# An eight-block transformer on one core: another order for the head loop's opening, a rectification shared by two engines, a top-54 threshold searched on unshifted scores

## The reference

```
# block 3, mLSTM: 16 heads, gates from a cumulated log-sigmoid
log_D = log_fg + ig                      # 256 x 256 per head, lower triangle
D = exp(log_D - max_log_D)
C = (q k^T / sqrt(dh)) * D
Cn = C / (max(|C.sum(-1)|, exp(-max_log_D)) + EPS)
h = Cn v                                 # then normalised per head
...
# block 7, attention over 256 keys, 54 scores kept
scores = coef * Q K^T
scores = scores - max(scores, -1)
thr = top_k(scores, 54)[0][..., -1:]
scores = where(scores < thr, -inf, scores)
out = softmax(scores) V @ W_o^T
...
# block 8, MLP with quantised activations and weights
h = bitlinear(h, w1)                     # 256 -> 1024
h = square(relu(h))
return bitlinear(h, w2)                  # 1024 -> 256
```

## Time and profile before

| | |
|---|---|
| median of 3 runs | 565.84 us (562.04 to 568.44) |
| the profiled execution's own time | 569.39 us |
| its span, first to last instruction | 567.7 us |
| mean granted TensorE clock | 0.901 |
| busy: PE, DVE, ACT, POOL | 461.2, 355.7, 234.0, 145.7 us |

### The profile page before, as it was taken

How to read it: one execution, slowest core, us unless ns; L and a number is a source line. 1 busy time by engine, 2 the same in 40 slices (tenths; PEclk the granted TensorE clock), 3 DMA queues, 4 the chain that set the end, 5 groups by cost and what they waited for, 6 DMA issues and landing times.

```text
span 567.7 us, 7522 instructions
## 1 busy us (share of the span) xinstructions
PE 461.2 (81%) x2709; PEld 339.5 (60%) x2718; DVE 355.7 (63%) x987; ACT 234.0 (41%) x422; POOL 145.7 (26%) x139
## 2 busy tenths in 40 slices
PE   1899989999999837779889689999887754766775
PEld 0688875557787625445556457788664533654544
DVE  6473456639314546695656668246478899799753
ACT  1200013532242715354543212423888643225896
POOL 4000010064854675433064555001000000010000
PEclk9999987999899968777798689999999996897978
DMA  8840260025894410001000200000000000000001
GB/s 269 273 186 1 72 224 1 1 68 193 307 286 133 145 53 17 7 5 38 0 1 2 76 1 1 1 0 1 0 2 0 1 1 0 2 1 0 10 29 38
DMA packets 21078, 34.70 MB, mean 61 GB/s; under 512 B 4935, under 2 KB 16074, under 8 KB 21040
## 3 DMA queue, kind: packets, MB, share of 16 engines
q1 hardware_dynamic: 18736, 30.23, 15.8%
q0 software_dynamic: 2304, 3.97, 2.5%
HBM read 32.32 MB, written 4.19 MB: 64 GB/s over the span
## 4 chain that ended last, share of the span: by engine, by line
PE 46%; DVE 30%; ACT 11%; POOL 6%; issue 5%; DMA 1%; DVEq 0%; POOLq 0%; ACTq 0%
PE bank L1516 5%; PE bank L1475 5%; PE bank L1485 5%; PE bank L1592 4%; PE bank L1847 3%; PE bank L1861 2%; DVE bnst L613 2%; DVE HN L623 2%; PE bank L1614 2%; DVE top L1137 2%; POOL ar L568 2%; DVE big L1134 2%; PE bank L1668 2%; DVE am L1019 2%; DVE X L824 1%
## 5 line engine op out<-in xcount | busy, mean ns | idle before, releaser
L471 POOL TENSOR_TENSOR rstd<-ve,neghalf 128x2 f32<-128x2 f32 x32 | 23.3, 729 | 270.0 <-DVE ve L618 269.9
L954 DVE TENSOR_TENSOR SH<-bank,HM 128x512 f32<-128x512 f32 x32 | 21.8, 688 | 23.2 <-ACT HM L1315 10.6
L1315 ACT ACTIVATE HM<-bank 128x512 f32<-128x512 f32 x32 | 19.1, 597 | 36.5 <-PE bank L1701 29.3
L623 DVE TENSOR_SCALAR HN<-X,mv,rstd 128x256 f32<-128x256 f32 x64 | 28.6, 488 | 7.8 <-POOL rstd L471 7.6
L1592 PEld LDWEIGHTS bank<-ph,big 128*128 128x128 f32 x256 | 31.9, 196 | 1.3 <-issue 0.4
L1475 PE MATMUL bank<-HM,CT 128*128 128x256 f32 x128 | 30.7, 403 | 1.2 <-DVE HM L647 1.2
L568 POOL TENSOR_TENSOR ar<-ar,neghalf 128x32 f32<-128x32 f32 x4 | 21.7, 5432 | 38.7 <-DVE ar L918 38.7
L1516 PE MATMUL bank<-HT,SH 128*128 128x512 f32 x64 | 31.6, 645 | 0.0
L1592 PE MATMUL bank<-ph,big 128*128 128x64 f32 x256 | 31.2, 276 | 0.0
L1475 PEld LDWEIGHTS bank<-HM,CT 128*128 128x128 f32 x128 | 26.0, 204 | 5.6 <-issue 1.5
L613 DVE BATCH_NORM_STATS2 bnst<-X 128x6 f32<-128x256 f32 x64 | 24.0, 418 | 7.6 <-POOL X L580 6.8
(11 more groups left out here) (364 smaller groups left out, 1160.7 us busy)
## 6 DMA issues: line engine op xcount, KB each, us to landing
big<-in_ew SPq DMA_DIRECT2D x16, 768.0 KB, 6.5
y_rows<-ph SPq DMA_DIRECT2D x16, 128.0 KB, 3.2
X<-in_x SPq DMA_DIRECT2D x4, 256.0 KB, 6.7
CT<-in_ctxT SPq DMA_DIRECT2D x1, 1024.0 KB, 7.7
CN<-in_ctx SPq DMA_DIRECT2D x1, 1024.0 KB, 11.4
ar<-in_q2g SPq DMA_DIRECT2D x1, 1024.0 KB, 4.9
ar<-in_q2u SPq DMA_DIRECT2D x1, 1024.0 KB, 7.1
big<-in_q2d SPq DMA_DIRECT2D x1, 1024.0 KB, 10.1
```

Of the source, the lines that this page charges most:

```text
L471: pool.tensor_tensor(rstd[:, b, :], ve[:, b, :], neghalf[:, 0:TB], ALU.pow)\
L623: last = dve.tensor_scalar(HN[:, TB * b + j, :], X[:, TB * b + j, :], mv[:, b, j, 0:1], rstd[:, b, j:j + 1], ALU.subtract, ALU.mult)
L954: dve.tensor_tensor(cs[:, g, :], bank[i % 3][:], dcs[:, i % 2, :], ALU.mult).then_inc(s["s_cs"], 1)
L1315: act.activation(dcs[:, i % 2, :], bank[4 + i % 2][:], ACT.Exp).then_inc(s["s_dexp"], 1)
```

## The change

There are three edits and a new order.

1. Opening of the head loop. `folded` 6 to 9 go ahead of the last weight sums, `tokens_turn(0)` and `token_gates(0)` on TensorE (and to the matching place on ACT). `gathered(3)` goes behind `part_rows(0)` on DVE. `compose_rows` copies each of the three pieces as soon as it is there, and goes ahead of `spread_rows(0)`, which moves behind the first `decays`, as `rows_turn(0)` moves behind the first `scores`. `weighted_values(0)` moves from round 0 to round 1.
2. `scores3` and `clip3`. DVE searches the unshifted scores. ACT takes the exp with the negated maximum as its bias, and then shifts `SC` in place, four instructions of 128 x 256 where there was one of 128 x 512; it may start when the first round has read `SC`. DVE shifts the threshold alone (128 x 2) and then waits for ACT before the mask.
3. `in3`. ACT rectifies the first 512 columns, DVE the other 512 from the other bank; a new step `max3` holds DVE's maximum and ACT's square.
4. All four strings of `TURNS_OF` are new.

```
 FFN3 = [((name, j), engines) for j in range(TB) for name, engines in
-        (("in3", "TVS"), ("round3", "S"), ("turn3", "TS"), ("out3", "TV"))]
+        (("in3", "TVS"), ("max3", "VS"), ("round3", "S"), ("turn3", "TS"), ("out3", "TV"))]
...
-    "V": ("00121200213123033221303011200321213030120123102032112030321231323203101320213302013213203123"),
+    "V": ("00121202031231022130301120303122010312012313202013123003213213020131323003213210213032201331212"
+          "32331023"),
...
             gathered(1)
             ln_stats(0)
+            token_norm(0)
+            gathered(2)
             dve.wait_ge(s["s_gc"], 1)
             weight_scales(4, 5)
-            token_norm(0)
-            gathered(2)
             gate_rows(0)
-            gathered(3)
             sum_rows(0)
             max_rows(0)
             part_rows(0)
+            gathered(3)
...
                 if step[0] == "in3":
-                    dve.wait_ge(s["s_gs"], nth("S", INS, step, b))
+
+                    dve.wait_ge(s["s_gu"], nth("T", INS, step, b))
+                    dve.tensor_scalar(GS[b][:, 512:1024], bank_b(b)[:], fg[:, TB * b + step[1], 0:1], 0.0, ALU.mult,
+                                      ALU.max).then_inc(s["s_gv"], 1)
+                if step[0] == "max3":
+                    dve.wait_ge(s["s_gv"], nth("V", IN3, ("in3", step[1]), b))
+                    dve.wait_ge(s["s_gs"], nth("S", INS, ("in3", step[1]), b))
                     hidden_scale(b, 1)
...
-                    link(dve.tensor_scalar(nmax2[:, b], top3[:, b, :, 0], -1.0, None, ALU.mult))
-                    for j in range(TB):
-                        dve.tensor_scalar(top3[:, b, j, :], top3[:, b, j, :], nmax2[:, b, j:j + 1], None, ALU.add)
-                    for j in range(TB):
-                        last = dve.tensor_scalar(SC[b][:, j, :], SC[b][:, j, :], nmax2[:, b, j:j + 1], None, ALU.add)
-                    last.then_inc(s["s_m3"], 1)
+                    dve.tensor_scalar(nmax2[:, b], top3[:, b, :, 0], -1.0, None, ALU.mult).then_inc(s["s_m3"], 1)
...
+                    link(dve.tensor_tensor(top3[:, b, :, 0], top3[:, b, :, at], nmax2[:, b], ALU.add))
                     dve.wait_ge(s["s_ex3"], nth("S", ["clip3"], step, b))
...
             for h in range(2):
                 magnitudes(4, h)
+            for b in range(B):
+                folded(2 + B + b, VC[b])
...
-                act.wait_ge(s["s_part"], min(b, 2) + 1)
                 for p in range(3):
+                    act.wait_ge(s["s_part"], 3 * min(b, 2) + p + 1)
                     last = act.activation(CMP[32 * p:32 * (p + 1), b, :], part[32 * b:32 * (b + 1), p, :], ACT.Copy)
...
-                    act.wait_ge(s["s_m3"], nth("V", ["scores3"], "scores3", b))
-                    act.activation(EX3[b], SC[b], ACT.Exp).then_inc(s["s_ex3"], 1)
+                    act.wait_ge(s["s_m3"], nth("V", CUTS, "clip3", b))
+                    for j in range(TB):
+                        act.activation(EX3[b][:, j, :], SC[b][:, j, :], ACT.Exp, bias=nmax2[:, b, j:j + 1])
+                    for j in range(TB):
+                        last = act.activation(SC[b][:, j, :], SC[b][:, j, :], ACT.Identity, bias=nmax2[:, b, j:j + 1])
+                    last.then_inc(s["s_ex3"], 1)
```

More of the change, by code:

```diff
@@ L399, in flamingo @@
         IN3 = [("in3", j) for j in range(TB)]
-        FULL = [("in2b", j) for j in range(TB)] + IN3
+        CUTS = ["scores3", "clip3"]
+        MAX3 = [("max3", j) for j in range(TB)]
+        FULL = [("in2b", j) for j in range(TB)] + MAX3
         INS = IN2 + [("in3", j) for j in range(TB)]
@@ L1133, in _ @@
                                 dve.wait_ge(s["s_vec"], done[j])
-                            done[j] = mark(dve.match_replace(WR[b][:, j, :], top3[:, b, j, :], src[:, j, :], LOWEST))
+                            last = dve.match_replace(WR[b][:, j, :], top3[:, b, j, :], src[:, j, :], LOWEST)
+                            if r >= 1:
+                                done[j] = mark(last)
+                        if r == 0:
+                            last.then_inc(s["s_m3"], 1)
+                            dve.wait_ge(s["s_m3"], nth("V", CUTS, "clip3", b))
                         for j in range(TB):
-                            dve.wait_ge(s["s_vec"], done[j])
+                            if r >= 1:
+                                dve.wait_ge(s["s_vec"], done[j])
                             done[j] = mark(dve.max(top3[:, b, j, :], WR[b][:, j, :]))
-                    dve.wait_ge(s["s_ex3"], nth("S", ["clip3"], step, b))
                     at = (CLIP - 1) % 8
@@ L1333, in _ @@
             log_rows(0)
-            for b in range(B):
-                folded(2 + B + b, VC[b])
             compose_rows(0)
-            spread_rows(0)
-            turned_rows(0)
             for i in range(4 * NO):
@@ L1342, in _ @@
                 decays(i)
+                if i == 0:
+                    spread_rows(0)
+                    turned_rows(0)
                 if i in (0, 5, 8):
@@ L1411, in _ @@
                     act.wait_ge(s["s_gu"], nth("T", INS, step, b))
-                    for n in range(2):
-                        last = act.activation(GS[b][:, 512 * n:512 * (n + 1)], bank[2 * b + n][:], ACT.Relu,
-                                              scale=fg[:, TB * b + step[1], 0:1])
-                    last.then_inc(s["s_gs"], 1)
-                    act.wait_ge(s["s_gs"], nth("S", INS, step, b))
+                    act.activation(GS[b][:, 0:512], bank_a(b)[:], ACT.Relu, scale=fg[:, TB * b + step[1], 0:1])\
+                        .then_inc(s["s_gs"], 1)
+                if step[0] == "max3":
+                    act.wait_ge(s["s_gs"], nth("S", INS, ("in3", step[1]), b))
+                    act.wait_ge(s["s_gv"], nth("V", IN3, ("in3", step[1]), b))
                     act.activation(H[b], GS[b], ACT.Square).then_inc(s["s_sq"], 1)
@@ L1789, in _ @@
                 folded(2 + b, weight(0), lambda k: CT[:, k, S * b:S * (b + 1)])
+            for b in range(B):
+                folded(2 + B + b, lambda k, m: CT[:, k, S * b + P * m:S * b + P * (m + 1)], lambda k: W2[:, 3, k, :])
             last_sums()
-            pe.wait_ge(s["s_ye"], ST)
-            pe.wait_ge(s["s_xsh"], B)
             tokens_turn(0)
             token_gates(0)
-            for b in range(B):
-                folded(2 + B + b, lambda k, m: CT[:, k, S * b + P * m:S * b + P * (m + 1)], lambda k: W2[:, 3, k, :])
-            rows_turn(0)
             pe.wait_ge(s["s_prec"], 2 + 2 * B)
```

35 lines of the change are left out of this document (21 added, 14 removed).

## The result

| | before | after |
|---|---|---|
| median of 20 runs each | 567.26 us (562.04 to 570.6) | 559.97 us (551.76 to 563.92) |
| ratio after to before | | 0.9843, 95% interval 0.98 to 0.9886 |
| the profiled execution, its span | 569.39, 567.7 us | 563.92, 562.2 us |
| mean granted TensorE clock | 0.901 | 0.888 |

The change makes the kernel 1.6% faster by the ratio, 8.9 us of 567.26; the forecast was 11.0. The ratio leaves out the runs more than 1.5% above the fastest of their kernel, nine of twenty after and three of twenty before. The medians of all twenty are 7.3 us apart, 1.3%. The profiled execution after is the slowest of the twenty, so its span alone says little; it is read stage by stage.

The account below looks back on a forecast made before the run. Bound in turn by TensorE (to 401 us), no engine (to 450.2), DVE with the searches, then ACT (last 43.50 us). Terms -2.6 - 2 - 0.4 - 6 = -11.0 gave 554.8 us against the median 565.84; predicted 555, range 547 to 566.

Parts of the forecast that it names:

- The opening: Head loop's opening: first exponents 3.65 us earlier, of which 2.6 is kept; term -2.6, bounds 0 and -3.7.
- `gate_rows(0)` ends at 212.99 before and after: Head loop's opening: this DVE step keeps its time, since it waits for gates that come from unmoved steps.
- Rival A: Head loop: the opening's gain is swallowed by later rounds, as by GpSimd's gathers; 557.4 us, chance 0.10.
- the gathers cost nothing: Head loop: GpSimd's last gather of tile 5 lands later, but 2.7 us of cover remain, so costed at nothing.
- The middle: 326.8 to 450.2 us: the new order wins back a quarter of the second stage's 8.12 us of TensorE idling; -2.
- rival C: Middle: longer waits lose TensorE's full clock, 0.70 in the second stage; kernel slower, 574.4 us, chance 0.10.
- The searches: 454.1 to 521.9 us: waits and score shifts leave DVE, other work and a new wait come; -0.4, bounds -4 and +6.6.
- The wait of 1.5 us at the first search: First search: DVE waits ahead of the mask for ACT's exp and shift; 1.5 us, bounds 0 and 5.
- The last stage: Last 43.5 us: ACT loses half of each tile's rectification and some earlier-done work; 37.5 us, -6, bounds 0 and -11.5.
- ACT has 32.0 left: Last stage: ACT's busy time falls from 39.24 us to 32.0.
- Rival B: Last stage: no gain, since DVE takes ACT's place in each tile's serial chain; 560.8 us, chance 0.20.
- E: Better case: opening and last stage reach their lower ends (-3.7, -11.5), with -2 and -0.4; 548.2 us, chance 0.10.

Follow-up runs that it names:

- e_fold_back: The kernel after with the last four folded products behind the gates on TensorE again, ACT's copies of them between the pieces: ratio 0.9762, one of three that flatter.
- e_no_half: The kernel after with both halves of the rectification on ACT again, new order kept without the added steps: ratio 0.9981 to before.
- e_opening: The kernel before with only the new opening of the head loop: ratio 0.9871 to before.
- e_order: The kernel before with only the four new order strings, without the digits of the split's added steps: ratio 1.0003 to before.
- e_half: The kernel before with only the rectification halved between ACT and DVE, old order, DVE's half right ahead of its maximum: ratio 1.0068 to before.
- e_half_early: The kernel before with the halved rectification, old order, DVE's half one step earlier in seven of eight tiles: ratio 0.9891, one of three that flatter.
- e_clip: The kernel before with only the search on unshifted scores, old order: ratio 1.0046 to before.
- e_half_late: The kernel after with DVE's half moved back behind another batch's addition or normalisation in four of eight tiles: ratio 0.9961 to before.
- e_old_order: The kernel before with all three edits in the old order, the split's steps put in at their places: ratio 1.0143 to before.

## Why the prediction was right, and where its sizes were off

**The opening: right, too small.** Forecast -2.6, measured -3.6: the stretch to the first search has a mean of 243.60 in the seven kernels with the new opening as it stands (241.38 to 245.54) and 247.19 in the six with the old one (246.40 to 248.07). At the loop's end the means are 109.27 and 112.34, -3.1; the other 0.5 arises behind the loop, where no edit of the opening stands, and is not explained. The step that failed is "`gate_rows(0)` ends at 212.99 before and after: it waits for the gates, which come from unmoved steps". Counted from the mark it begins at 6.88 before (212.31) and 6.21 after (210.59). TensorE had been idle for 3.5 us ahead of `tokens_turn(0)`, not 7.53, since `folded` filled the place, and the four products took 0.66, not 1.09. The rows of before, then the gates of after, then e_fold_back, where `folded` is out of that place again and the products take 1.12:

```profile
207.13 1.09 PE L1657 MATMUL bank<-identf,HN 128*128 128x128 f32 x4 [7.53 <-DVE HN L623]
...
212.31 0.68 DVE L837 TENSOR_TENSOR WK<-bank,ex 32x512 f32<-32x512 f32 x1 [3.09 <-PE bank L1668]
```

```profile
210.59 0.68 DVE L840 TENSOR_TENSOR WK<-bank,ex 32x512 f32<-32x512 f32 x1 [2.08 <-PE bank L1687]
```

```profile
204.58 1.12 PE L1678 MATMUL bank<-identf,HN 128*128 128x128 f32 x4 [6.12 <-DVE HN L626]
```

The other steps held: `sum_rows` stands 2.05 behind `gate_rows` (212.64 - 210.59), not 2.75, the 0.7 of the forecast; `tokens_turn(1)` waits for DVE; the gathers cost nothing. Apart from `folded`, the moves of the opening were not run one by one.

**Rival A came in part.** In two of these seven, after and e_no_half, the loop ends 110.86 and 111.07 us behind the mark, where the other five have a mean of 108.60: 2.3 and 2.5 us were given back in the head loop, not to the gathers but to the clock. Windows at the same distance from the mark, in after, in before and in e_opening:

```profile
275.20:291.20 16.00, 16.00 (x101) 9.28 (x98) 6.85 (x15) 4.03 (x8) 8.54 (x4) 0.50 0.00 1
```

```profile
276.25:292.25 16.00, 15.78 (x139) 10.16 (x140) 8.55 (x19) 9.72 (x19) 5.26 (x1) 0.79 0.00 1
```

```profile
268.55:284.55 16.00, 15.88 (x144) 10.12 (x136) 8.53 (x19) 6.22 (x12) 9.04 (x4) 0.84 0.00 1
```

TensorE is full in all three, but in after it gets through 101 products instead of 139 to 144, at the lower level (1.2 GHz). In this window the clock is 0.50 in three of the eight kernels with a new opening (after, e_no_half, e_fold_back), 0.80 to 0.87 in the other five, and 0.68 to 0.79 in the six with the old one. So the new opening doesn't lose it each time; what decides it stays open.

**The middle: wrong, -2 forecast, nothing measured.** e_order ends it at 247.11 against 246.40, within the spread of the kernels with the old opening. From the loop's end to the first maxima the eight kernels with the new order take 134.5 us on the mean, and the six with the old one 134.6. TensorE's busy time hardly changed (41.08 to 41.68), and rival C didn't come: the clock is 1.00. The error was to give an order a gain that no row priced.

**The searches: about right in sum, and by luck: -0.4 forecast, +0.6 measured** (68.36 against 67.80, the mean of before, e_opening, e_half and e_half_early). The shift's edit gives 0.8 in the new order, while the new order alone costs 0.9 to 1.7 there, for the work that it moves in. In the profiled pair the parts are off in opposite directions. I had DVE's waits fall by 2.0 (-3.48 + 1.5) and its work grow by 1.6; its idle time in this stage went from 4.97 to 5.18 and its work from 62.99 to 63.52 (the windows of before and after are below). The two old waits left, but two others came (1.6 for ACT's silu in the second MLP, 1.3 for the shift). The wait of 1.5 us at the first search did not come: ACT's shift ended before DVE wanted the mask. The windows from the first maxima to the fourth mask, before and after:

```profile
451.83:519.79 67.96, 41.80 (x175) 31.92 (x176) 62.99 (x236) 23.35 (x36) 2.88 (x4) 0.80 0.00 1
```

```profile
449.74:518.44 68.70, 45.94 (x199) 33.82 (x198) 63.52 (x230) 36.57 (x57) 2.87 (x4) 0.78 0.00 1
```

ACT's timeline after:

```profile
455.31 0.69 ACT L1452 ACTIVATE big<-bank,coef 128x512 f32<-128x512 f32 x1
456.02 1.28 ACT L1456 ACT_TABLE_LOAD   x1
457.31 0.91 ACT L1456 ACTIVATE big<-big,nmax 128x256 f32<-128x256 f32 x2
458.13 0.89 ACT L1458 ACTIVATE big<-big,nmax 128x256 f32<-128x256 f32 x2
```

and DVE's masks of the first and the third search:

```profile
459.90 0.88 DVE L1156 SCALAR_TENSOR_TENSOR big<-big,top 128x256 f32<-128x256 f32 x2
...
503.51 0.88 DVE L1156 SCALAR_TENSOR_TENSOR big<-big,top 128x256 f32<-128x256 f32 x2 [1.32 <-ACT big L1458]
```

The pairs took 0.91 and 0.89, less than the 1.09 that I had from the nearest row, and the first search won with 0.9 us to spare. The wait came at the third, where I had ACT idle: its queue had been held by copies that wait for TensorE, 9.31 and 3.87 us, the last until 498.82. A switch of tables again cost 1.29 (456.02 to 457.31). By the Trainium skill ("ScalarE: Activation LUTs", What ACT_TABLE_LOAD costs) a drain of 1.38 would have come on top. By that figure, as an estimate, the first mask would have waited about half a us; the trace has neither.

**The last stage: right, slightly too large.** Forecast -6, measured -5.0: a mean of 40.36 in the five kernels with the halves in the new order as in after, against 45.37 (before, e_opening, e_order, e_clip). e_no_half shows that it is the halves, e_half_late that it is their place. "ACT has 32.0 left" was near (30.99), but in after's window ACT idles 8.6 us (39.60 - 30.99), where I had 5.5 (4.3 + 1.2). Rival B is the true danger, and what I gave against it, that four batches run against each other, is not what decides: with the same four batches it came true in e_half and e_old_order, and its price there was not zero but +5. In the new order it depends on where DVE's half stands beside the additions that wait for TensorE, which DVE's order would have shown.

Summed up: -3.6 + 0 + 0.6 - 5.0 = -8.0 by stages, 8.9 by the ratio (6.5 to 11.3), 7.3 by the medians, 11.0 forecast. Of the 3.0 us between the forecast and the stages the middle makes 2.0, the searches and the last stage 1.0 each, and the opening takes 1.0 back. Two slips in the prediction move nothing: the lower bound of the search term adds up to -4.6, not -4, and the range is said to take in most of E and also to leave half of it out.

## What to carry to other kernels

Work that is split between two engines paid here only where the helper's part stood ahead of the helper's own waits; count the waits of the first engine for the second in the place where it will stand, not only the sums of busy time. A new order is worth nothing or a good deal depending on the edits it is written for: e_order alone 1.0003, the three edits without it 1.0143, together 0.9843. And where the part ahead of a change doesn't always end at the same time, measure stages from a mark behind it.

## What was not expected of the chip

The granted clock of TensorE differs between executions of the same instructions. Blocks 1 and 2 are the same code in all kernels here, yet batch 0's power began at 205.43 in before, 204.38 in after and 197.41 in e_order. Windows in block 1, in before and in e_order:

```profile
76.00:80.00 4.00, 2.11 (x16) 1.73 (x15) 2.75 (x9) 1.08 (x2) 0.79 (x1) 1.00 0.66 223
...
84.00:88.00 4.00, 4.00 (x18) 3.48 (x18) 1.38 (x4) 0.00 (x0) 0.00 (x0) 0.50 0.00 0
```

```profile
76.00:80.00 4.00, 2.12 (x16) 1.73 (x15) 2.74 (x9) 1.09 (x2) 0.79 (x1) 1.00 0.65 224
...
84.00:88.00 4.00, 4.00 (x16) 2.10 (x15) 3.65 (x14) 0.00 (x0) 0.00 (x0) 1.00 0.00 0
```

TensorE is idle for the same 1.9 us in both, to a hundredth; then one execution drops to the lower level until about 92 us, and the other doesn't. In all fourteen traces this wait is 1.88 or 1.89 us. In nine of them the clock from 84 to 88 us is 0.50 and batch 0's power begins at 202.82 to 205.43; in the other five it is 1.00 and the power begins at 197.41 to 199.65. The block's later steps came some 5 us apart (the first gather at 115.90 against 110.92). This fits the spread of before's runs, from 562 to 571 us, but only profiled executions can be read this way. No edit here touches this code.
